# A prediction kernel for click rates on one core: tile 3's fifteenth table turned on its own, the last run of tile 2's Gram matrices and the pairs of tile 2 moved in TensorE's order

## The reference, cut to what matters

```
e = stack([tbl_k[ids[:, k]] for k in 26 tables], axis=1)        # 512 x 26 x 128
all_emb = concatenate([bottom[:, None, :], e], axis=1)            # 512 x 27 x 128
gram = einsum('bfd,bgd->bfg', all_emb, all_emb)
z = gram[:, i, j]  for the 351 pairs i < j
h = relu(concatenate([z, bottom], axis=1) @ W_top1 + b_top1)      # 479 -> 512
h = relu(h @ W_top2 + b_top2)                                     # 512 -> 256
y = h @ W_top3                                                    # 256 -> 1
```

## Time and profile before

| what | us |
|---|---|
| three runs | 101.61, 101.35, 101.37 |
| median | 101.37 |
| the profiled execution, its own time | 101.67 |
| span of its instructions | 99.9 |
| PE busy | 94.6 |
| DVE, ACT, POOL busy | 60.0, 55.7, 60.4 |

### The profile page before, as it was taken

How to read it: one execution, slowest core, us unless ns; L and a number is a source line. 1 busy time by engine, 2 the same in 40 slices (tenths; PEclk the granted TensorE clock), 3 DMA queues, 4 the chain that set the end, 5 groups by cost and what they waited for, 6 DMA issues and landing times.

```text
span 99.9 us, 3533 instructions
## 1 busy us (share of the span) xinstructions
PE 94.6 (95%) x1512; PEld 82.0 (82%) x1512; DVE 60.0 (60%) x152; ACT 55.7 (56%) x95; POOL 60.4 (60%) x63
## 2 busy tenths in 40 slices
PE   4999999999999999999999999999999698999992
PEld 4798778888888888888899888979899587998981
DVE  3499999999999997986793044007400091047010
ACT  3798578959899999984962022421424035212232
POOL 2678778777877778777787777777777700000000
PEclk9999999999999999999999999999999999999999
DMA  1897999559687564699722222222222210000000
GB/s 40 257 355 237 365 369 339 203 162 322 225 261 208 197 228 81 173 227 261 241 59 53 59 57 54 59 57 54 57 54 57 54 33 7 0 7 3 0 7 1
DMA packets 6414, 13.70 MB, mean 137 GB/s; under 512 B 1907, under 2 KB 2691, under 8 KB 6398
## 3 DMA queue, kind: packets, MB, share of 16 engines
q1 hardware_dynamic: 4406, 9.66, 28.5%
q0 software_dynamic: 1824, 3.74, 15.1%
q10 hardware_dynamic: 168, 0.07, 0.3%
HBM read 13.45 MB, written 0.01 MB: 135 GB/s over the span
## 4 chain that ended last, share of the span: by engine, by line
PE 89%; issue 4%; ACT 4%; DVE 1%; POOL 0%; ACTq 0%
PE acc L644 36%; PE acc L705 12%; PE acc L739 11%; PE ring L684 6%; PE acc L672 6%; PE ring L750 5%; PE acc L730 4%; PE acc L603 3%; PE acc L617 2%; PE ring L763 2%; PE ring L713 1%; ACT emb L425 1%; ACT onehot L399 1%; PE ring L774 1%; ACT far L378 1%
## 5 line engine op out<-in xcount | busy, mean ns | idle before, releaser
L347 POOL DMA_INDIRECT rows<-tbl,ids_sb x57 | 59.8, 1049 | 18.7 <-issue 17.1
L533 DVE TENSOR_SCALAR onehot<-far 128x512 fp32r<-128x512 f32 (+2 forms) x85 | 29.8, 407 | 1.7 <-ACT far L378 1.7
L644 PE MATMUL acc<-onehot,hi 128*128 128x512 f32 (+1 forms) x84 | 23.3, 401 | 0.0
L644 PE MATMUL acc<-onehot,lo 128*128 128x512 f32 (+1 forms) x84 | 22.0, 386 | 0.0
L555 DVE STREAM_TRANSPOSE pairs<-acc 128x832 f32<-128x832 f32 x4 | 4.2, 1050 | 25.3 <-PE acc L705 25.3
L644 PEld LDWEIGHTS acc<-onehot,lo 128*128 128x128 f32 x84 | 15.7, 188 | 3.2
L644 PEld LDWEIGHTS acc<-onehot,hi 128*128 128x128 f32 x84 | 15.1, 192 | 3.5 <-DVE onehot L533 0.8
L519 DVE TENSOR_TENSOR lo<-raw,hi 128x512 fp32r<-128x512 f32 (+1 forms) x24 | 16.8, 701 | 1.9 <-ACT hi L364 1.9
L364 ACT CAST hi<-raw 128x1024 fp32r<-128x1024 f32 (+1 forms) x11 | 12.0, 1091 | 6.1 <-issue 3.7
L463 ACT COPY emb<-ring 128x512 f32<-128x512 f32 (+2 forms) x16 | 8.9, 556 | 11.4 <-PE ring L684 11.2
L705 PE MATMUL acc<-emb 128*27 128x27 f32 x1024 | 12.8, 193 | 1.7 <-issue 0.9
(11 more groups left out here) (53 smaller groups left out, 74.2 us busy)
## 6 DMA issues: line engine op xcount, KB each, us to landing
raw<-looked SPq DMA_DIRECT2D x9, 512.0 KB, 4.7
raw<-looked SPq DMA_DIRECT2D x2, 640.0 KB, 5.4
ids_b<-ids SPq DMA_DIRECT2D x4, 256.0 KB, 5.5
rows<-tbl,ids_sb POOLq DMA_INDIRECT x57, 4.1
w1z<-w SPq DMA_DIRECT2D x3, 234.0 KB
raw<-looked SPq DMA_DIRECT2D x2, 256.0 KB, 3.4
w_sb<-w SPq DMA_DIRECT2D x1, 512.0 KB
bot<-bottom_t SPq DMA_DIRECT2D x1, 256.0 KB, 7.2
```

What stands on the lines that cost most here:

```text
L347: nc.gpsimd.indirect_dma_start(out=rows[:, t, slot, :], out_offset=None, in_=tables[table], in_offset=bass.IndirectOffsetOnAxis(ap=ids_sb[ ...
L533: ins = nc.vector.tensor_scalar(onehot[:, n % OH_RING, k, of], far[:, t % FAR_RING, of], float(KP * c), None, ALU.is_equal)
L644: mm = nc.tensor.matmul(acc[:, look_bank(t), 0:looked_up(t)], part_of[:, t % HL_RING, c * D:(c + 1) * D], onehot[:, n % OH_RING, k, 0:look ...
```

## The change

- `work_order`: the run (16, 32) of tile 2's Gram goes from ahead of "l1 1,3" to behind "l1 1,3", "l2 1" and "turn 3,2". "bottom 3,0" goes from behind "pairs 3" to ahead of tile 3's first Gram run. "pairs 2" goes from ahead of that run to behind it, directly ahead of "l1 2,0".
- Tile 3's slot NG becomes a turn of its own, "turn 3,4", which stands behind "bottom 3,0" and ahead of tile 3's Gram. It is transposed into the `acc` bank that "bottom 3,1" uses later and waits for all of tile 1's h1. ACT copies it by itself. "turn 3,3" keeps two slots.
- ACT's one-hot of the last table's first chunk is made in the step "compare" of table 10, right behind its `far`, and no longer in the step "compare" of table 11.

```diff
+def turns_of(t):
+
+    return TURNS + (t >= FIRST_TILES)
+
+
 def group(t, g):
 
-    slots = GROUPS[g]
-    return range(slots[0], NG + 1) if g == TURNS - 1 and t >= FIRST_TILES else slots
+    return range(NG, NG + 1) if g == TURNS else GROUPS[g]
...
               ("part", NL - 1, 3), ("gram", 1, (0, 12)), ("pairs", 0, 0), ("bottom", 1, 0), ("turn", 2, 2), ("l1", 0, 0),
               ("l1", 0, 1), ("gram", 1, (12, 32)), ("bottom", 1, 1), ("l1", 0, 2), ("l1", 0, 3), ("turn", 2, 3),
               ("l2", 0, 0), ("pairs", 1, 0), ("gram", 2, (0, 12)), ("turn", 3, 0), ("l1", 1, 0), ("bottom", 2, 0),
-              ("gram", 2, (12, 16)), ("turn", 3, 1), ("l1", 1, 1), ("l1", 1, 2), ("gram", 2, (16, 32)), ("l1", 1, 3),
-              ("l2", 1, 0), ("turn", 3, 2), ("bottom", 2, 1), ("turn", 3, 3), ("pairs", 2, 0), ("gram", 3, (0, 20)),
-              ("l1", 2, 0), ("l1", 2, 1), ("l1", 2, 2), ("gram", 3, (20, 32)), ("l1", 2, 3), ("l2", 2, 0),
-              ("pairs", 3, 0), ("bottom", 3, 0), ("bottom", 3, 1), ("l1", 3, 0), ("l1", 3, 1), ("l1", 3, 2),
+              ("gram", 2, (12, 16)), ("turn", 3, 1), ("l1", 1, 1), ("l1", 1, 2), ("l1", 1, 3), ("l2", 1, 0), ("turn", 3, 2),
+              ("gram", 2, (16, 32)), ("bottom", 2, 1), ("turn", 3, 3), ("bottom", 3, 0), ("turn", 3, 4),
+              ("gram", 3, (0, 20)), ("pairs", 2, 0), ("l1", 2, 0), ("l1", 2, 1), ("l1", 2, 2), ("gram", 3, (20, 32)),
+              ("l1", 2, 3), ("l2", 2, 0), ("pairs", 3, 0), ("bottom", 3, 1), ("l1", 3, 0), ("l1", 3, 1), ("l1", 3, 2),
               ("l1", 3, 3), ("l2", 3, 0), ("l2", 3, 1), ("columns", 0, 0), ("l3", 3, 0)]
     return order
 
 
 ORDER = work_order()
-USES = [s for s in ORDER if s[0] in ("turn", "pairs", "l2", "columns", "l3")]
+USES = [s for s in ORDER if s[0] in ("turn", "pairs", "l2", "columns", "l3") and s != ("turn", LAST, TURNS)]
...
-        rows_in = [[sem(f"rows_in{t}_{g}") for g in range(TURNS)] for t in range(TILES)]
+        rows_in = [[sem(f"rows_in{t}_{g}") for g in range(turns_of(t))] for t in range(TILES)]
...
-                for g in range(TURNS):
+                for g in range(turns_of(t)):
...
+            def first_chunk(j):
+                n = 2 * j
+                act.wait_ge(far_ready, j + 1)
+                if n >= OH_RING:
+                    act.wait_ge(oh_used, n - OH_RING + 1)
+                nc.scalar.activation(onehot[:, n % OH_RING, 0, 0:looked_up(j)], far[:, j % FAR_RING, 0:looked_up(j)],
+                                     ACT.Relu, bias=1.0, scale=-1.0).then_inc(oh_act, 1)
...
-                    act.wait_ge(far_ready, t + 1)
-                    if n >= OH_RING:
-                        act.wait_ge(oh_used, n - OH_RING + 1)
-                    nc.scalar.activation(onehot[:, n % OH_RING, 0, 0:looked_up(t)], far[:, t % FAR_RING, 0:looked_up(t)],
-                                         ACT.Relu, bias=1.0, scale=-1.0).then_inc(oh_act, 1)
+                    if t < NL - 1:
+                        first_chunk(t)
...
+                    if t == NL - 2:
+                        first_chunk(NL - 1)
...
-                    b = bank(step, t, part)
                     slots = group(t, part)
                     n = len(slots)
-                    nc.scalar.copy(emb[:, t, :, slots[0]:slots[0] + n],
-                                   ring[:, b, 0:n * LANES].rearrange("d (p f) -> d p f", f=n)
+                    of = ring[:, bank(step, t, part), 0:n * LANES] if part < TURNS else acc[:, top_bank(2 * LAST + 1), 0:LANES]
+                    nc.scalar.copy(emb[:, t, :, slots[0]:slots[0] + n], of.rearrange("d (p f) -> d p f", f=n)
                                    ).then_inc(emb_turned, 1)
...
-                b = bank(step, t, part) if step in ("turn", "pairs", "l2", "columns", "l3") else None
+                b = bank(step, t, part) if (step, t, part) in USES else None
...
-                    wait_emptied(step, t, part)
                     slots = group(t, part)
+                    if part < TURNS:
+                        wait_emptied(step, t, part)
+                        into = ring[:, b, 0:len(slots) * LANES]
+                    else:
+
+                        pe.wait_ge(h1_ready, M1 // 2 * (2 * LAST + 1 - TOP + 1))
+                        into = acc[:, top_bank(2 * LAST + 1), 0:LANES]
                     pe.wait_ge(rows_in[t][part], 16 * len(slots))
-                    turn = ring[:, b, 0:len(slots) * LANES].rearrange("d (p f) -> d p f", f=len(slots))
+                    turn = into.rearrange("d (p f) -> d p f", f=len(slots))
...
-                        pe.wait_ge(emb_turned, turn_count(t, TURNS - 1))
+                        pe.wait_ge(emb_turned, turn_count(t, turns_of(t) - 1))
```

## The result

The changed kernel takes 102.34 us (median of 4 runs, 102.12 to 102.47) against 101.36 for the one before: a ratio of 1.0113, 95% interval 1.0069 to 1.0157 (the two medians alone give 1.0097). It is slower by about 1%, as forecast (102.4). In a later series the ratio was 1.0100 (1.0071 to 1.0128). The sum was right, but by luck in part: two of its terms were far off, and what they missed nearly cancelled with changes that the forecast didn't have.

The account below looks back on a forecast made before the run. PE, busy 94.6 of 99.9 us, bounds the kernel, so only its idle time counts. Terms -0.29 + 0.27 + 1.05 + 0 = +1.03 on the median 101.37 give 102.4 us, bounds 102.1 to 103.1; stated range 101.3 to 103.1.

Parts of the forecast that it names:

- The pairs of tile 2 ahead of layer 1: PE stands still during ACT's copy to `zt`: 1.28 from first transpose to layer 1, net +1.05 us.
- The 0.2 that should come back in layer 1: Tile 2's 18 layer-1 matmuls, 2.21 behind a Gram run, would take 2.01 us otherwise.
- The term of +1.05: Net cost in us of tile 2's pairs directly ahead of "l1 2,0"; bounds +0.95 and +1.28.
- The one-hot: Last table's first chunk: PE's wait for ACT near 49.3 goes and the gain carries through, -0.29 us.
- The stretch to tile 3's Gram: From 75.33 to the start of tile 3's Gram: 8.66 against 8.39 us, +0.27, bounds +0.2 and +0.45.
- the 0.93: PE's pause in us at 77.67 inside tile 2's Gram run (16, 32), without a program wait; the forecast kept it.
- its own sign: Prediction is wrong if the 0.93 us pause is absent, or pairs to layer 1 takes under 0.9 us.
- "bottom 3,0" and the split: Tail change 0, as layer 1 waits some 0.4 us for `zt`; splitting ACT's copy ahead of tile 3's Gram wins 0.05.
- pause gone: Rival: tile 2's Gram pause comes from the instruction stream and goes; sum +0.10, 101.5 us (101.3 to 101.9), chance 0.23.

Follow-up runs that it names:

- the shift: The kernel before with 16 more matmuls of 27 x 27 (64 recorded PE instructions) in PE's warm-up near 6 us; 105.62 us, ratio 1.043.
- the run with more work over DVE's transposes: Changed kernel without the split, "turn 3,2" behind tile 2's last Gram run, pairs of tile 2 after 12 lane groups of tile 3's Gram; 102.56 us, ratio 1.014.

## Why the prediction was right, and where it was right by luck

- **The pairs of tile 2 ahead of layer 1: right.** Forecast 1.28 from the first transpose to layer 1, measured 1.21 in the changed kernel and in the run with this move alone, which makes +1.1% by itself. The 0.2 that should come back in layer 1 didn't (2.20): I had put the 0.2 down to the Gram run ahead of it, but it was there behind the pairs too. Half of it can be what stands behind: twelve layer-1 matmuls take 1.44 up to a Gram run (75.33 to 76.77) and 1.34 up to a turn (68.08 to 69.42). The term of +1.05 is also 0.03 less than its own 1.28 - 0.20.
- **The one-hot: wrong.** The step "behind it PE works without a gap that a wait explains, so the gain should carry through" failed. The wait went, and the next dense run gave it back in the changed kernel (1.23 to 1.48); the run with this edit alone has the same longer run and no gain in time (ratio 0.9994). The mis-sized term is -0.29; it measured +0.08 in the profiles.
- **The stretch to tile 3's Gram: wrong, by the pause.** I kept the 0.93 in the sum. It was a refill of PE's instructions at a fixed count and left this run, as the rival had it (with a chance of 0.23); -0.86 in place of +0.27. By its own sign ("I am wrong if the 0.93 is absent") the prediction's account of this stretch failed, though its number held. Of the rest the reading held: without the pause the sum was 8.66 - 0.93 = 7.73, measured 7.53; the 0.2 between them are in the run itself, 1.20 where I had 1.39 (0.09 less on the way from "turn 3,4" to the Gram and 0.09 more at "turn 3,2" cancel). DVE and ACT release tile 3's Gram at nearly the same time (DVE ends at 82.05 + 0.57 = 82.62, ACT at 82.40 + 0.39 = 82.79, PE starts at 82.94), as worked out, although DVE began 0.19 behind the Gram run and not 0.36.
- **Where the pause would go was not foreseen.** It stood one block later, in tile 3's first run (+0.57), and a small one at the start of its second run went (-0.20). In length of the runs, 1.12 and 0.20 before became 0.57, a gain of 0.75 that the forecast didn't have.
- **The errors nearly cancel.** Measured less forecast: front +0.37, the stretch -1.13, tile 3's first run +0.57 and second -0.20, layer 1 +0.19, pairs -0.04. That is -0.24: forecast +1.03, profiles +0.79, medians +0.98.
- **"bottom 3,0" and the split: right in the time, not wholly in the reasons.** Layer 1 of tile 3 waits for `zt` anyway, but the wait is 0.18 and not some 0.4. For the split I had priced ACT's copy at 0.05 and held that the gathers are not in the way. Without the split the last gather costs 0.42, and tile 3's Gram starts 0.25 later; the block boundary in that run takes it back.
- **The rival "pause gone" was right in its mechanism, wrong in its end.** Its argument against ("tile 3's run of 160 matmuls is as dense and has none") is answered by the count: in the old order the boundary there was passed at 84.16 by count, 5.5 us after the one at 78.60, and the block had arrived at 81.06. The Trainium skill's rule that the buffer holds 2,048 instructions and that crossing a block is mostly hidden ("Runtime: NRT & Kernel Launch", Instruction fetch mechanics) does not agree with these runs, as far as the crossing goes: boundaries stopped PE for 0.2 to 2.2 us. How deep the buffer is no run shows. Its block of 256 instructions agrees.

The net of the parts: the pairs alone cost 1.1%, and the place of the Gram run is worth 0.6 to 1.0 us within the changed kernel. The changed kernel is nonetheless 1% slower than before, because with the Gram run in its old place it is slower still than the pairs alone make it (103.18 against 102.49). By the profiles 0.45 of that is tile 3's Gram, which starts at 84.28 there and at 83.83 with the pairs alone: 0.37 of it arises behind the pause, where "bottom 3,0" stands ahead of the Gram, and 0.08 up to the pause's end (78.89 against 78.81).

## What to carry to other kernels

A copy between two steps of the same engine needs something of its own length between them: put transposes one run ahead of their consumer, and split a long run if need be. When one engine issues very many small instructions, count them, its waits too: here a pause that no semaphore explained and that stayed at the same instruction count when the work was moved was the instruction supply. Then look when the blocks arrive, on the instruction queue of the DMA view. Such an order has to be judged by how the dense runs are spaced as well as by the sum of its steps. A few instructions added far ahead can cost more than any move nearby, and a gain just ahead of a boundary may not carry past it.

## What the runs showed of the hardware that was not expected

- PE's instruction stream comes in blocks of some 16 KB and, with its waits counted, exactly 256 instructions (pauses at 2241 and 2497, with the shift at 1729, 1985 and 2753). PE went on 1.3 to 1.6 us behind the end of the block's packet, at all twelve such pauses that have a row of their own (0.19 to 2.18 us long). In four of the five pauses of the table PE reached the boundary 1.3 to 3.4 us behind the one before and went on 2.7 to 4.1 us behind it. The fifth opened after 5.6 us, with a late packet, and in the run with more work over DVE's transposes a boundary is passed without a pause 3.4 us behind the last. The spacing alone is no rule. What sets when a packet begins stays open. The length of a pause at the same place differs between executions (0.46, 0.69, 0.93 and 1.21 in four profiles with the same order up to there), which may go with the spread of the times (100.5 to 101.9 for the kernel before).
- 16 matmuls of 27 columns, 62 to 83 us ahead of the places where PE then paused, cost 4.4 us; 64 of them, which fill a whole block, cost 3.5, none of it at the boundaries.
- Shorter pauses of 0.2 to 0.3 us within the Gram runs of tiles 0 and 1 (1.23 or 1.48 for a run that takes 0.93 in tile 2) don't lie at the boundaries, and their counts differ from profile to profile (660 in the kernel before, 606 and 676 in the changed one, with the boundary at 671). Their cause stays open; in the changed kernel they gave back what the one-hot had won.
